# Windowed attention in a two-layer transformer block: computing the never-visible key blocks of each sequence's first two tiles, under loaded masks, instead of leaving them out

## The reference, cut to what matters

```python
bk, bv = (look_around(bk), look_around(bv))      # the window before, then the own one
sim = jnp.einsum('bhwid,bhwjd->bhwij', bq, bk)
mask = (i < j) | (i > j + WINDOW) | (j == -1)    # j == -1: padding before the first window
sim = jnp.where(mask, -jnp.finfo(sim.dtype).max, sim)
attn = jax.nn.softmax(sim, axis=-1)
out = jnp.einsum('bhwij,bhwjd->bhwid', attn, bv)
```

## Time and profile before

| | |
|---|---|
| median of 3 runs | 3728.22 us (3725.76 to 3728.98) |
| the profiled execution | 3725.76 us, of which the span from first to last instruction is 3724.0 us |
| mean granted clock of PE | 0.971 of full speed |
| busy share of the span | PE 94%, PE weight loads 76%, DVE 61%, ACT 40%, POOL 32% |
| the DMA engines | 67 GB/s on average |
| attention stage, layer 0 | from about 653 us to about 1405 us of the span |
| attention stage, layer 1 | from about 2187 us to about 2940 us |

### The profile page before, as it was taken

How to read it: one execution, slowest core, us unless ns; L and a number is a source line. 1 busy time by engine, 2 the same in 40 slices (tenths; PEclk the granted TensorE clock), 3 DMA queues, 4 the chain that set the end, 5 groups by cost and what they waited for, 6 DMA issues and landing times. The chain is left out here.

```text
span 3724.0 us, 56508 instructions
## 1 busy us (share of the span) xinstructions
PE 3486.6 (94%) x20624; PEld 2821.9 (76%) x20624; DVE 2267.6 (61%) x5002; ACT 1504.1 (40%) x3973; POOL 1177.3 (32%) x1036
## 2 busy tenths in 40 slices
PE   5889987799999997999999969999999699999998
PEld 4666665688888875888888858888888588888887
DVE  5776775699999984322332239999999642322221
ACT  4655663455555553111111125555555421111111
POOL 2333342555555531111111125555555111111111
PEclk8999999899999998999999989999999899999999
DMA  5111122212121114111111121211111231111111
GB/s 132 39 42 54 56 76 70 92 61 64 60 63 58 58 51 139 66 63 63 63 63 62 52 103 51 63 59 58 58 58 56 89 112 62 63 63 63 63 62 52
DMA packets 215591, 249.21 MB, mean 67 GB/s; under 512 B 32761, under 2 KB 142594, under 8 KB 215317
## 3 DMA queue, kind: packets, MB, share of 16 engines
q1 hardware_dynamic: 215317, 245.61, 20.3%
HBM read 138.17 MB, written 90.61 MB: 61 GB/s over the span
## 5 line engine op out<-in xcount | busy, mean ns | idle before, releaser
L1674 DVE SCALAR_TENSOR_TENSOR u_full<-banks,b_cols,gate 128x512 f32<-128x512 f32 (+1 forms) x176 | 132.1, 751 | 890.8 <-ACT gate L1616 793.2
L45 PE MATMUL banks<-fxT_h,w_h 128*128 128x512 f32 (+1 forms) x1408 | 558.3, 397 | 5.2 <-DVE fxT_l L1666 5.2
L47 PE MATMUL banks<-fxT_h,w_l 128*128 128x512 f32 (+1 forms) x1408 | 557.3, 396 | 0.0
L46 PE MATMUL banks<-fxT_l,w_h 128*128 128x512 f32 (+1 forms) x1408 | 556.5, 395 | 0.0
L1616 ACT ACTIVATE gate<-banks,b_cols 128x512 f32<-128x512 f32 (+1 forms) x176 | 121.3, 689 | 1028.8 <-PE banks L47 1028.8
L1010 POOL TENSOR_TENSOR rn<-ssq,neg_half 128x8 f32<-128x8 f32 x128 | 210.8, 1647 | 410.7 <-DVE ssq L1282 404.2
L45 PE MATMUL banks<-wqkv_h,hT_h 128*128 128x512 f32 x768 | 323.3, 421 | 16.1 <-DVE wqkv_l L1269 16.1
L1323 DVE TENSOR_SCALAR prob<-prob,rc 128x384 f32<-128x384 f32 (+2 forms) x512 | 315.6, 658 | 9.1
L45 PEld LDWEIGHTS banks<-fxT_h,w_h 128*128 128x128 f32 (+1 forms) x1408 | 260.3, 185 | 75.7 <-DVE fxT_l L1666 11.1
L1218 ACT ACTIVATE pT_h<-banks 128x384 fp32r<-128x384 f32 (+2 forms) x512 | 213.7, 469 | 254.3 <-PE banks L1107 253.5
L47 PEld LDWEIGHTS banks<-fxT_h,w_l 128*128 128x128 f32 (+1 forms) x1408 | 261.2, 186 | 67.6
(11 more groups left out here) (170 smaller groups left out, 8195.4 us busy)
## 6 DMA issues: line engine op xcount, KB each, us to landing
y_in<-y_rows SPq DMA_DIRECT2D x64, 256.0 KB, 2.9
z_rows<-y_in SPq DMA_DIRECT2D x64, 256.0 KB, 2.0
f_res<-z_rows SPq DMA_DIRECT2D x16, 1024.0 KB, 5.6
f_x<-x_rows SPq DMA_DIRECT2D x16, 1024.0 KB, 8.0
y_rows<-f_res SPq DMA_DIRECT2D x16, 1024.0 KB, 4.3
out_rows<-f_x SPq DMA_DIRECT2D x16, 1024.0 KB, 4.8
w_ffn_stage<-in_w SPq DMA_DIRECT2D x30, 512.0 KB, 4.9
x_in<-in_x SPq DMA_DIRECT2D x10, 1024.0 KB, 6.7
```

The costliest lines, as they stand in the source:

```text
L45: pe.matmul(out, a_h, b_h, start=start, stop=False)
L46: pe.matmul(out, a_h, b_l, start=False, stop=False)
L47: return pe.matmul(out, a_l, b_h, start=False, stop=stop)
L1674: e.scalar_tensor_tensor(out=u_full[r, m % 2, :], in0=ps[r, 2 * (m % 2), :], scalar=b1[r, m, 0:1], in1=gate[r, :], op0=ALU.add, op1=ALU.mu ...
```

## The change

The first two tiles of each sequence are treated like all others. All three key blocks are computed everywhere, `first_block` and `seen` are gone, and the blocks that no query may see are hidden by the mask. For that, masks for tiles with `t % 4` of 0 or 1 are loaded from a table for each group of four tiles (`load_masks`, two DMAs of 128 x 256 fp32, 8 times a layer) into a new tile `mask01`, whose last 128 columns of each slot come by two more small loads at the start of the stage. The key and value slots that tile 0 would read before anything was written there are zeroed by POOL (four memsets of 1024 fp32 a partition), and SP, PE, ACT and DVE each wait for `pl_init` once a stage.

```diff
+        mask01 = sb("mask01", [P, 2, KEYS])
-        def first_block(t):
-            return max(2 - t % (N // P), 0)
-        def seen(t):
-            return slice(first_block(t) * P, KEYS)
+                def load_masks(i):
+                    for u in range(2):
+                        r = i * 2 * P + u * P
+                        e.wait_ge(s["dv_s"], at(LH, i, 4 * HEADS, -2 * HEADS))
+                        e.dma_start(mask01[:, u, 0:2 * P], io["mask01"][bass.ds(r, P), :]).then_inc(s["ld_mask"], 16)
...
+                        if u == 2 and i < NI - 1:
+                            load_masks(i + 1)
                         store(i, u - 1)
...
                 e.dma_start(mask[:], io["mask"]).then_inc(s["ld_small"], 16)
+                for u in range(2):
+                    e.dma_start(mask01[:, u, 2 * P:KEYS], io["mask"][:, 2 * P:KEYS]).then_inc(s["ld_small"], 16)
                 load_tables(0, 0)
                 load_h(0, 1)
                 load_weights(w.slots, w.count)
                 load_h(0, 2)
                 load_tables(0, 1)
+                load_masks(0)
+                e.wait_ge(s["pl_init"], 4 * l + 4)
...
+                for part in range(2):
+                    e.memset(kT[part][:, :, 0:2, :].bitcast(F32), 0.0).then_inc(s["pl_init"], 1)
+                    e.memset(v[part][:, 2:4, :].bitcast(F32), 0.0).then_inc(s["pl_init"], 1)
...
-                            last = e.matmul(ps[:, 2 + odd, seen(t)], qT[a][r, t % 2, p, :],
-                                            kT[b][r, p, t % 4 + first_block(t):t % 4 + 3, :].rearrange("p a k -> p (a k)"),
+                            last = e.matmul(ps[:, 2 + odd, 0:KEYS], qT[a][r, t % 2, p, :],
+                                            kT[b][r, p, t % 4:t % 4 + 3, :].rearrange("p a k -> p (a k)"),
...
-                    for k in range(first_block(t), 3):
+                    for k in range(3):
                         last = e.transpose(ps[:, 4 + h % 2, k * P:(k + 1) * P], prob[:, n % 4, k * P:(k + 1) * P], ident[:])
...
-                    for k in range(first_block(t), 3):
+                    for k in range(3):
                         slot = (t + 2 + k) % 4
...
+                        if h == 0 and t % 4 == 0:
+                            e.wait_ge(s["ld_mask"], 32 * (l * NI + t // 4 + 1))
...
-                        e.tensor_tensor_reduce(out=neg_s[:, n % 4, seen(t)], in0=ps[:, 2 + h % 2, seen(t)], in1=mask[:, seen(t)], scale=-1.0,
+                        mk = mask01[:, t % 4, :] if t % 4 < 2 else mask[:]
+                        e.tensor_tensor_reduce(out=neg_s[:, n % 4, :], in0=ps[:, 2 + h % 2, 0:KEYS], in1=mk, scale=-1.0,
```

More of the change, by code:

```diff
@@ L826, in attention_sems @@
     s = {n: [sem(f"a_{n}{u}") for u in range(4)] for n in ("ld_h", "ld_rot", "ld_y", "st")}
-    for n in ("ld_small", "k_copy", "dv_own", "pe_h", "ac_h", "dv_h", "pe_qkv", "ac_sq", "dv_ssq", "pl_rn", "dv_norm",
+    for n in ("ld_small", "ld_mask", "k_copy", "dv_own", "pe_h", "ac_h", "dv_h", "pe_qkv", "ac_sq", "dv_ssq", "pl_rn", "dv_norm",
               "pl_tab", "pl_m1", "pl_m2", "pl_rot", "ac_v", "dv_v", "pe_r", "ac_r", "dv_r", "pe_s", "dv_s", "ac_exp", "dv_rc", "dv_p",
-              "pe_t", "ac_t", "dv_t", "pe_o", "ac_o", "dv_o", "pe_w", "dv_y"):
+              "pe_t", "ac_t", "dv_t", "pe_o", "ac_o", "dv_o", "pe_w", "dv_y", "pl_init"):
         s[n] = sem(f"a_{n}")
@@ L984, in _ @@
                 e.dma_start(dram["dst_late"][N:N + 1, :], zero_row[:]).then_inc(s["ld_small"], 16)
-                e.wait_ge(s["ld_small"], 16 * 8 * l + 16 * 8)
+                e.wait_ge(s["ld_small"], 16 * 10 * l + 16 * 10)
             def token_major_heads(ap):
@@ L991, in _ @@
             def _(e):
-                e.wait_ge(s["ld_small"], 16 * 8 * l + 16 * 7)
+                for part in range(2):
+                    e.memset(kT[part][:, :, 0:2, :].bitcast(F32), 0.0).then_inc(s["pl_init"], 1)
+                    e.memset(v[part][:, 2:4, :].bitcast(F32), 0.0).then_inc(s["pl_init"], 1)
+                e.wait_ge(s["ld_small"], 16 * 10 * l + 16 * 9)
                 def rotate(i, j):
@@ L1121, in values @@
                                             [x[:, slot, h * DH:(h + 1) * DH] for x in v],
-                                            [x[:, n % 4, k * P:(k + 1) * P] for x in pT], k == first_block(t), k == 2)
+                                            [x[:, n % 4, k * P:(k + 1) * P] for x in pT], k == 0, k == 2)
                     last.then_inc(s["pe_o"], 1)
@@ L1210, in exponent @@
                         e.wait_ge(s["dv_p"], nth(LH, n - 3))
-                        e.activation(prob[:, m, seen(t)], neg_s[:, m, seen(t)], ACT.Exp, bias=neg_m[:, m:m + 1], scale=-1.0,
+                        e.activation(prob[:, m, :], neg_s[:, m, :], ACT.Exp, bias=neg_m[:, m:m + 1], scale=-1.0,
                                      accum_out=sm[:, m:m + 1]).then_inc(s["ac_exp"], 1)
@@ L1217, in hi_p @@
                     e.wait_ge(s["pe_o"], nth(LH, n - 3))
-                    e.activation(pT[0][:, n % 4, seen(t)], ps[:, 4 + h % 2, seen(t)], ACT.Copy).then_inc(s["ac_t"], 1)
+                    e.activation(pT[0][:, n % 4, :], ps[:, 4 + h % 2, 0:KEYS], ACT.Copy).then_inc(s["ac_t"], 1)
                 def hi_o(t, half):
@@ L1322, in divide @@
                         for m in (n % 4, n % 4 + 1):
-                            e.tensor_scalar(prob[:, m, seen(t)], prob[:, m, seen(t)], rc[:, m:m + 1], None, ALU.mult).then_inc(s["dv_p"], 1)
+                            e.tensor_scalar(prob[:, m, :], prob[:, m, :], rc[:, m:m + 1], None, ALU.mult).then_inc(s["dv_p"], 1)
                 def lo_p(t, h):
@@ L1327, in lo_p @@
                     e.wait_ge(s["ac_t"], nth(LH, n + 1))
-                    e.tensor_tensor(pT[1][:, n % 4, seen(t)], ps[:, 4 + h % 2, seen(t)], pT[0][:, n % 4, seen(t)].bitcast(F32),
+                    e.tensor_tensor(pT[1][:, n % 4, :], ps[:, 4 + h % 2, 0:KEYS], pT[0][:, n % 4, :].bitcast(F32),
                                     ALU.subtract).then_inc(s["dv_t"], 1)
```

## The result

The changed kernel takes 3766.66 us (median of 6 runs, 3761.07 to 3770.39) against 3728.76 us for the kernel before in 6 runs: ratio 1.0100, 95% interval 1.0087 to 1.0112. A later series of both gave 3763.38 against 3730.17 us, ratio 1.0093 (1.0079 to 1.0107). It is slower by 33 to 38 us (the two intervals reach from 29 to 42); 3765 us had been forecast.

The account below looks back on a forecast made before the run. PE was taken to bound the attention tiles, DVE close behind. Second sequence 17.0, first sequence 17.8 and loads 2.2 gave +37.0 us; with 2.46 for the median 3765 us, 1.0% slower, range 3755 to 3774 (forecast's own 3759 to 3771, chance 0.76).

Parts of the forecast that it names:

- PE sets the pace in full tiles: Attention stages: PE sets 22.72 us a tile; filling tiles 16 and 17 costs +8.51 us a layer.
- The estimate from single instructions: Tiles 16 and 17: 0.33 us a block and head, 24 of them 7.9 us, kept as the lower end.
- next in line: Full attention tiles: DVE is busy 1.32 us a tile less than PE's 22.72 and stays below PE.
- The first sequence costs about the same: Tiles 0 and 1 at the stage start: 8.51 plus 0.35 of net gap growth, 8.9 us a layer, bounds 4.6 to 12.5.
- the four gaps: PE's idle gaps at the stage start: first two grow some 0.6 us, third some 0.3, fourth (0.56) goes away.
- The new loads: Stage start: two more issues on SP's queue delay everything behind by 0.96 us; 1.1 us a layer, bounds 0 and 2.
- The start hides its part: Rival, chance 0.08: start idle time is filled, loads cost nothing, PE gets full clock there (5.3 us); +22, 3750 us.
- Nothing changes: Rival, chance 0.03: tiles around 16 and 17 were short for another cause; only the loads' 2.2 us remain, 3730 us.
- Faster: Rival, chance 0.02: zero blocks keep PE active across stage starts, and a higher clock gives back over 37 + 7.5 us.
- The start costs more: Rival, chance 0.11: gaps grow by the full chain, lower clock lasts through more of tile 0; +48, 3776 us.
- a lower clock alone: Start stretches before the change: the same instructions took 1.52 us longer in layer 1 (31.65 against 30.13) by clock.
- Costed at nothing: Four memsets (3.7 us, covered by POOL's idle time), `pl_init` waits, later mask loads and their waits: no cost.

Follow-up runs that it names:

- ten slots: Kernel with the change's loads, memsets and waits alone, its two small loads cut into ten of the same bytes: 3735.81 us, ratio 1.0020.
- the two half runs: Changed kernel with blocks left out as before in tiles 0 and 1 (3744.39 us), or in tiles 16 and 17 (3746.54 us).

## Why the prediction was right

**PE sets the pace in full tiles, and the added blocks are paid at PE's rate.** Right, to the hundredth: +8.51 or +8.52 a layer in the second sequence, in both profiles of the changed kernel, in the run with that sequence alone, and, at 90.87 us, in the run where PE alone had the extra work. The estimate from single instructions, 7.9, was 0.6 low; the difference of two whole stretches was the better source. The run with DVE's and ACT's share alone corrects one sentence: DVE isn't merely "next in line". Its extra work alone would have cost 6.2 us a layer, so taking the blocks from PE only would win back just 2.3 of the 8.5.

**The first sequence costs about the same.** The forecast was 8.9 us a layer, from the first scores to the second full tile. Over the six starts that compute all blocks, first scores to residual 0 took 37.23 us on average (35.65 to 38.50), over the eighteen that leave them out 30.46 (30.01 to 31.89); with 1.10 for the next two pitches that is 7.9. Taken only where the clock was 0.94 or 0.95, the difference is 37.3 - 30.1 = 7.2, with the two pitches 8.3. The forecast was 0.6 to 1.0 too high. At that clock PE's busy time in the start grew by 7.0 us and its idle time by 0.2; with the two pitches PE's part is 8.1, where 8.51 was taken over from mid-layer. In layer 0 of the first profile the four gaps went as said in sign: two grew, by 0.34 together and not 0.6, the third by 0.36 and not 0.3, the fourth closed.

**The new loads: the step that failed.** "I take 1.1 us a layer": measured 0, within a few tenths by which the starts scatter. In the five profiles with two more slots, layer 0's first scores come after 38.3 to 38.8 us, in the four of unchanged queue order after 38.5 to 38.8; in layer 1 the means are 38.1 and 37.9. It was put as "That is not hidden", from the idle times of ACT and PE behind the weights. An idle engine behind a load shows that the load is late, not that it would be later by each issue slot ahead of it. Over the ten starts with two more slots the first value weight piece was issued 10.8 us after the stage's first issue on average, over the eight of unchanged order 9.8; it landed after 15.6 in both. The slack is in the transfers: in the changed kernel's layer 0 the four value pieces were issued 0.47 us apart and landed 0.67 apart, behind what was already on its way. Only when ten slots had used that wait up did the start come 3 us later.

**The sum.** The terms as measured are 17.0 + 15.7 + 0 = 32.7 us, where 37.0 were forecast. The medians moved by 37.9 and 33.2 us. So the near hit of 3765 owes something to chance: the terms are 4 us smaller than forecast, and the first series lay some 5 us higher than they explain. Both series' intervals, 32 to 42 and 29 to 40 us, hold 32.7 and 37.0 alike. The profiles show where one program differs from itself by that much. In the last three residuals of a layer, which are full tiles in every kernel, 24 cases took between 31.46 and 36.89 us, with granted clocks from 1.00 down to 0.81, in kernels of both kinds:

```profile
1372.84:1408.93 36.09, 27.90 (x207) 22.52 (x206) 21.34 (x60) 15.27 (x42) 0.00 (x0) 0.81 0.14 45
```

That is the run with loads alone, whose median equals the kernel before, though this execution was its slowest. PE's longest gap there is 1.75 us in all twelve profiles. The unedited kernel scatters as well: in one series its executions reach from 3722.11 us at a mean clock of 0.973 to 3734.51 at 0.967. But only two of them are profiled, and these have the shortest ends of layer 0, 31.48 and 33.01 us against 33.81 to 36.89 in the ten others. So it isn't excluded that any edit, the change too, moves this end a little; no run tests it. The Trainium skill ("TensorE: Matmul & The Clock Gate", section on the clock gate) says that the clock is throttled by default and released by activity, and that at a kernel's start the point of the change varies from run to run. That it varies in mid-kernel too is what these traces show: 0.86 and 1.00 for the same stretch, layer 1's end, in two executions of the changed kernel.

**The rivals.** "The start hides its part" is out: PE's idle time there is as long as before. Its clock part shows in one of six starts, layer 1 of the first profile, at 35.65 us with clock 1.00, so it exists and is worth 1.5 to 2 us there. "Nothing changes" is out by the two half runs and by the run of PE's share. "Faster" had too little to give back. "The start costs more" didn't occur; the longest start was 38.50. Its argument put the 1.52 us between the two starts of the kernel before down to "a lower clock alone"; 0.20 of them are idle time, 3.37 against 3.17.

**Costed at nothing, rightly:** memsets, the waits for them, the 14 later mask loads and the waits for them, by the run with loads alone. No run took the memsets' cover away.

## What to carry to other kernels

If a kernel already holds both forms of a piece of work, here tiles with and without skipped blocks, cut the trace at the same event in both and take the difference of whole stretches; it beat a sum of single instructions and needs no model of overlap. Ask for each engine's share alone before calling one the bound: two engines at 100% and 94% each brought most of the same price, and the prices overlap instead of adding up. A wait at the end of a chain of loads shows neither what one more issue slot costs nor what an earlier load brings; compare each load's issue with its landing, and try the order, since the load next in line may be only a little behind.

## What the runs showed of the hardware that was not expected

The same stretch of work, at a stage's end where PE has gaps of about a microsecond, ran at granted clocks of 0.81 to 1.00 and took 31.5 to 36.9 us over all kernels, and 31.5 and 36.0 us in two executions of one program, while stretches without gaps repeated to 0.03 us in all twelve profiles (residual 2 to 14: 272.63 to 272.66). And two further DMA issues of 0.48 us ahead of the weights cost nothing, because the weights then waited 0.8 us less behind earlier transfers (6.4 and 5.6 us from issue to landing in layer 0), while eight more, without more bytes, cost 3.2 and 3.0 us of 3.8, with 3.4 us from issue to landing.
